# Macaron: rotated q and k are summed into the buffer that is transposed and scaled there in place; the normed tile in a two-tensor form

## The chip, the cores and the metric

The kernel runs on one core of a Trainium2 chip. The metric is the device time of one execution in microseconds. TensorE (PE), VectorE (DVE), ScalarE (ACT), GpSimd (POOL) and SyncE (SP) each work through their own instructions in order, and meet only at semaphores.

## The reference, cut to what matters

Six stages follow each other on x of shape 2 x 1024 x 128. Two of them, the first and the third, are the "macaron" stage, x + 0.5 * f(layernorm(x)), and the change is inside it. f is six layers of local attention with a gated feed-forward unit:

```python
for i in range(DEPTH):                                   # 6
    x = attn_layer(shift_tokens(x), Wqkv[i], q_scale[i], k_scale[i], Wo[i]) + x
    x = ffn_layer(shift_tokens(x), ln_g[i], ln_b[i], W1[i], b1[i], W2[i], b2[i]) + x

def attn_layer(x, Wqkv, qs, ksc, Wo):
    q, k, v = split(x @ Wqkv)                            # 16 heads of 64
    q, k = l2norm(q) * qs, l2norm(k) * ksc
    q = q * cos * scale + rotate_half(q) * sin * scale
    k = k * cos * inv + rotate_half(k) * sin * inv
    return local_attention(q, k, v) @ Wo                 # windows of 32, one back

def ffn_layer(x, g, bln, W1, b1, W2, b2):
    xn = (x - mean) / sqrt(var + 1e-05) * g + bln
    a, gate = split(xn @ W1 + b1)
    return a * gelu(gate) @ W2 + b2
```

The other four stages (linear attention, experts, softmax attention, experts) are not touched.

## The kernel before

All of x lies in SBUF, as 16 tiles of 128 tokens x 128 features. A macaron stage is one software pipeline over 96 tiles (6 layers x 16 tiles). It takes 106 steps, s = -3 to 102, and each engine has its part of `step(s)` written out by hand. In step s the engines work on several tiles at once: u = s+2 is projected to q and k and rotated, k = s+1 has its q and k transposed and its v projected, t = s goes through the softmax, o = s-1 is weighed and projected out, z = s-4 is normed for the feed-forward unit. Of each four steps three carry feed-forward matmuls for a group of four tiles (gate, up, out).

The life of q and k of one tile, with the lines of the kernel before:

- TensorE projects four pieces of 512 columns, q in pieces 0 and 1, k in pieces 2 and 3 (`project_qk`). ScalarE squares each (L534).
- VectorE rotates each piece with two multiplications by the tables (`rotate`, L640), into `turn1` and `turn2`. Piece 3 of the next tile comes behind the transposes of this one on TensorE (`turn_qk(k, 0)`, `attend(o, 1)`, `project_qk(u, 3)`).
- GpSimd adds `turn2` to `turn1`, once for q and once for k (`add`, L751).
- VectorE sums the squares (`lengths`, L645) and writes a first guess of the inverse root (L711). GpSimd refines it in twelve small instructions (`rsqrt`, L760 to L766).
- GpSimd multiplies `turn1` by these roots into `qkr` (`scale`, L744), in the next step; TensorE transposes `qkr` (`turn_qk`, L367) in four parts, 0 and 1 for q, 2 and 3 for k. Parts 1 and 2 follow each other, and `project_v` (L356) goes before part 1 and before part 3.

There is one `turn1`, `turn2` and `qkr` for q and one for k. So `rotate` of the next tile waits until `scale` has read `turn1` (semaphore `qk_rotated`), and `scale` waits until `qkr` of the tile before is transposed (`qk_turned`). L711 also waits for `scale`, since it overwrites the roots. GpSimd's order in a step is: scale q, scale k, add q, divide the softmax by its sums (L780), add k, then `rsqrt`.

The normed tile `zn` of the feed-forward unit is written by two VectorE instructions of 128 x 64 (L685 and L687), (x - mean) * root, with mean and root as one value per partition. They stand ahead of `lengths`, and so ahead of L711.

Of the kernel before, what the change touches and what calls it, by code (L numbers as in the profile page):

```python
# [13 lines left out]
ALU = mybir.AluOpType  # L14
# [7 lines left out]
P = 128  # L22
D = 128
HALF = D // 2
# [3 lines left out]
TILES = BATCH * TPB  # L28
DEPTH = 6
HEADS = 16  # L30
DH = 64
RH = DH // 2
# [9 lines left out]
LN_EPS = 1e-5  # L42
# [13 lines left out]
def slot(t):  # L56
# [8 lines left out]
             qk_rotated=2, p_turned=2, pT_kept=2, aT_kept=2, unit_gate=3, unit_up=3, gelu=3, gated=3)  # L65
# [6 lines left out]
class Counts:  # L72
# [5 lines left out]
    def part(self, n, name, i=0):  # L78
        return PARTS.get(name, 1) * (self.macaron * NT + n) + i + 1
# [17 lines left out]
def build(nc, x_in, W, const, maskc, out):  # L97
    with ExitStack() as ctx:
        def sb(name, shape, dt=F32):
            return ctx.enter_context(nc.sbuf_tensor(name, shape, dt))  # L100
# [3 lines left out]
        def sem(name):  # L104
            if name not in sems:
                sems[name] = ctx.enter_context(nc.semaphore(name))
            return sems[name]
# [6 lines left out]
        Y = sb("Y", [P, TILES, D])  # L114
# [6 lines left out]
        maskf = sb("maskf", [P, 2, NWIN])  # L121
        half = sb("half", [P, 32])
        eps = sb("eps", [P, TILES])
        spare = sb("spare", [P, 1])

        wqkv = [sb(f"wqkv{i}", [P, 3 * INNER]) for i in range(2)]
# [10 lines left out]
        turn1 = sb("turn1", [P, 2, 2, HEADS, RH])  # L137
# [81 lines left out]
        def bc(ap, n):  # L219

            return ap.unsqueeze(2).broadcast_to([ap.shape[0], ap.shape[1], n])
# [88 lines left out]
        def on(n):  # L310
            return 0 <= n < NT
# [301 lines left out]
        def macaron_dve(dve, c):  # L613
# [15 lines left out]
            def rotate(n, q):  # L629

                w, a = q // 2, q % 2
                dve.wait_ge(sem("squared"), part(n, "squared", q))
                if on(n - 1) and a == 0:
                    dve.wait_ge(sem("qk_rotated"), part(n - 1, "qk_rotated", w))
                src = bank[QK_BANK[q]][:, :].rearrange("p (h d) -> p h d", d=RH)
                for tr in range(2):
                    dst = (turn1[:, w, a, :, :], turn2[:, w, 1 - a, :, :])[tr]
                    i = a ^ tr
                    tab = ropes[:, 2 * w + tr, n % TPB, RH * i:RH * i + RH]
                    e = dve.tensor_tensor(dst, src, tab.unsqueeze(1).broadcast_to([P, HEADS, RH]), ALU.mult)  # L640
                e.then_inc(sem("turned"), 1)
# [6 lines left out]
            def step(s):  # L648
# [33 lines left out]
                if on(z):  # L682
                    if on(z - 1):
                        dve.wait_ge(sem("mixed"), mixed(s - 1))
                    dve.tensor_scalar(zn[:, 0:HALF], Y[:, z % TILES, 0:HALF], mv[:, 0:1], rn[:, 32:33], ALU.subtract,  # L685
                                      ALU.mult)
                    dve.tensor_scalar(zn[:, HALF:D], zs[:, z % 3, :], mv[:, 0:1], rn[:, 32:33], ALU.subtract,  # L687
                                      ALU.mult).then_inc(sem("unit_normed"), 1)
                if on(u):
                    lengths(u, 0)  # L690
                if on(v):
# [5 lines left out]
                    lengths(u, 1)  # L697
                if on(v):
                    dve.wait_ge(sem("unit_moments"), part(v, "unit_moments"))
                    dve.tensor_scalar(ss[:, 32:33], mv[:, 1:2], LN_EPS, None, ALU.add).then_inc(sem("unit_var"), 1)  # L700
                if on(u):
                    dve.wait_ge(sem("summed"), part(u, "summed", 1))
                    dve.tensor_scalar(ss[:, 0:32], ss[:, 0:32], 1e-24, None, ALU.max).then_inc(sem("norms_squared"), 1)
                    dve.wait_ge(sem("norms_squared"), part(u, "norms_squared"))
                if on(v):
                    dve.wait_ge(sem("unit_var"), part(v, "unit_var"))
# [28 lines left out]
        def macaron_pool(pool, c):  # L735
            at = Counts(c)
            part, mixed = at.part, at.mixed

            def scale(n, w):
                r = rn[:, 16 * w:16 * w + 16]  # L740
                pool.wait_ge(sem("added"), part(n, "added", w))
                if on(n - 1):
                    pool.wait_ge(sem("qk_turned"), part(n - 1, "qk_turned", 2 * w + 1))
                pool.tensor_tensor(qkr[:, w, :].rearrange("p (h a d) -> p a h d", a=2, d=RH), turn1[:, w, :, :, :],  # L744
                                   r.unsqueeze(1).unsqueeze(3).broadcast_to([P, 2, HEADS, RH]),
                                   ALU.mult).then_inc(sem("qk_rotated"), 1)

            def add(n, w):
                pool.wait_ge(sem("turned"), part(n, "turned", 2 * w + 1))
                t1 = turn1[:, w, :, :, :].rearrange("p a h d -> p (a h d)")  # L750
                pool.tensor_tensor(t1, t1, turn2[:, w, :, :, :].rearrange("p a h d -> p (a h d)"), ALU.add).then_inc(  # L751
                    sem("added"), 1)

            def rsqrt(s):
                n0 = NEWTON * (at.step(s) - 1)
                pool.wait_ge(sem("guessed"), at.step(s))
                for i in range(3):
                    if i:
                        pool.wait_ge(sem("newton"), n0 + 4 * i)
                    pool.tensor_tensor(rt[:, :], rn[:, :], rn[:, :], ALU.mult).then_inc(sem("newton"), 1)  # L760
                    pool.wait_ge(sem("newton"), n0 + 4 * i + 1)
                    pool.tensor_tensor(rt[:, :], rt[:, :], ss[:, :], ALU.mult).then_inc(sem("newton"), 1)  # L762
                    pool.wait_ge(sem("newton"), n0 + 4 * i + 2)
                    pool.tensor_scalar(rt[:, :], rt[:, :], -0.5, 1.5, ALU.mult, ALU.add).then_inc(sem("newton"), 1)
                    pool.wait_ge(sem("newton"), n0 + 4 * i + 3)
                    pool.tensor_tensor(rn[:, :], rn[:, :], rt[:, :], ALU.mult).then_inc(  # L766
                        sem("newton" if i < 2 else "rnorm"), 1)

            def step(s):
                u, k, t = s + 2, s + 1, s  # L770
                if on(k):
                    pool.wait_ge(sem("rnorm"), at.step(s - 1))
                    scale(k, 0)
                    scale(k, 1)
                if on(u):
                    add(u, 0)
                if on(t):
                    pool.wait_ge(sem("inverted"), part(t, "inverted"))
                    pv = prob[:, :].rearrange("p (h k) -> p h k", k=NWIN)
                    pool.tensor_tensor(pv, pv, bc(rden[:, :], NWIN), ALU.mult).then_inc(sem("normalised"), 1)  # L780
                if on(u):
                    add(u, 1)
                rsqrt(s)

            for s in range(FIRST_STEP, FIRST_STEP + STEPS):
                step(s)
# [615 lines left out]
        def _(dve):  # L1402
# [2 lines left out]
            dve.memset(gT[:, 2, :], 1.0)  # L1405
            dve.memset(half[:, :], -0.5)
            dve.memset(eps[:, :], LN_EPS)
            dve.memset(ones[:, :], 1.0)
            dve.wait_ge(sem("const_loaded"), LOADS)
            dve.tensor_copy(identb[:, :], ident[:, :])  # L1410
# [110 lines left out]
```

## Time and profile before

| What | Value |
|---|---|
| Median of 3 runs | 4565.99 us (4559.22 to 4576.77) |
| Time of the profiled execution | 4562.12 us |
| Its span | 4560.3 us |
| PE busy | 3990.9 us (88%) |
| DVE busy | 3449.5 us (76%) |
| POOL busy | 2695.7 us (59%) |
| ACT busy | 2640.0 us (58%) |
| Chain that ended last, by engine | PE 37%, DVE 33%, POOL 15%, issue 11%, ACT 3% |

How to read it: the share of busy time is that of the whole span. TensorE's matmuls are pipelined and their ends are modelled, so 88% does not say that TensorE sets the pace. The chain that ended last goes back from the last instruction, at each step to what released it. "issue" is time in which an engine waited for nothing that the profile shows. PEclk is the clock that TensorE was granted, as a share of 2.4 GHz. In rows of the timeline the columns are start (us), duration (us), engine, line, operation, output and inputs, count; a bracket tells how long the engine sat idle before and what ended that.

### The profile page before, as it was taken

What the parts mean: (1) busy time and instruction counts of PE and PEld (TensorE: products, weight loads), DVE (VectorE), ACT (ScalarE), POOL (GpSimd) and SP (SyncE); (2) the same over time, 40 slices, a digit from 0 to 9 for tenths busy, and PEclk for the clock granted to TensorE, in tenths of its full rate; (3) what the DMA queues carried; (4) which work ended last, traced back from release to release, by engine and by line L of the source; (5) the groups of instructions that cost most, each with busy time, mean ns of one, the idle gap of its engine ahead of it and who ended that gap; (6) DMA issues with size and microseconds to landing.
All of it is one profiled execution on the core that took longest, in us unless ns stands there. A gap on an engine that the chain in (4) does not pass through costs nothing.

```text
span 4560.3 us, 162200 instructions
## 1 busy us (share of the span) xinstructions
PE 3990.9 (88%) x70897; PEld 2461.2 (54%) x70897; DVE 3449.5 (76%) x5613; ACT 2640.0 (58%) x4548; POOL 2695.7 (59%) x3554
## 2 busy tenths in 40 slices
PE   4899999999999998569999999999999985899975
PEld 2566656566665656335666666565656653333333
DVE  5888888888888887468888888788888854676744
ACT  3666666666666665046666666666666641266651
POOL 4777777777777776277777777677777750100000
PEclk8999999999999999789999999999999987699996
DMA  3000000000000000000000000000000000000000
GB/s 80 5 4 24 9 23 5 9 24 9 5 24 9 23 5 9 20 3 9 4 23 9 23 4 9 23 10 23 5 9 4 5 4 0 0 1 1 1 1 9
DMA packets 75875, 53.53 MB, mean 12 GB/s; under 512 B 49048, under 2 KB 71976, under 8 KB 73520
## 3 DMA queue, kind: packets, MB, share of 16 engines
q1 hardware_dynamic: 75184, 43.29, 3.7%
q8 instruction: 560, 9.18, 0.8%
q14 instruction: 131, 1.07, 0.1%
HBM read 35.93 MB, written 1.05 MB: 8 GB/s over the span
## 4 chain that ended last, share of the span: by engine, by line
PE 37%; DVE 33%; POOL 15%; issue 11%; ACT 3%; DVEq 1%; POOLq 0%; SPq 0%; DMA 0%; ACTq 0%
DVE turn L640 12%; DVE zn L687 5%; POOL qkr L744 5%; PE psum L345 5%; PE psum L412 4%; DVE ss L645 4%; PE psum L367 3%; PE psum L1159 3%; PE psum L356 3%; PE psum L433 3%; DVE den L669 3%; POOL rt L762 2%; POOL rn L766 2%; POOL rt L760 2%; PE psum L1128 2%
## 5 line engine op out<-in xcount | busy, mean ns | idle before, releaser
L640 DVE TENSOR_TENSOR turn<-psum,ropes 128x512 f32<-128x512 f32 x1536 | 945.3, 675 | 306.3 <-POOL qkr L744 259.5
L751 POOL TENSOR_TENSOR turn<-turn 128x1024 f32<-128x1024 f32 x384 | 907.8, 2364 | 191.6 <-DVE turn L640 191.3
L345 PE MATMUL psum<-wqkv,xT 128*128 128x512 f32 x1536 | 813.8, 654 | 10.9 <-DVE turn L640 8.3
L534 ACT ACTIVATE sq<-psum 128x512 f32<-128x512 f32 x768 | 455.9, 594 | 618.1 <-PE psum L345 617.9
L744 POOL TENSOR_TENSOR qkr<-turn,rn 128x1024 f32<-128x1024 f32 x384 | 726.4, 1912 | 15.1
L367 PEld LDWEIGHTS psum<-ident,qkr 128*128 128x128 f32 x3072 | 340.0, 145 | 440.4 <-issue 158.3
L412 PEld LDWEIGHTS psum<-scratch,V 32*64 32x64 f32 x29952 | 409.6, 139 | 304.0 <-issue 302.5
L412 PE MATMUL psum<-scratch,V 32*64 32x64 f32 (+1 forms) x29952 | 461.1, 236 | 112.6 <-issue 71.7
L367 PE MATMUL psum<-ident,qkr 128*128 128x128 f32 x3072 | 479.2, 291 | 90.0 <-POOL qkr L744 87.3
L760 POOL TENSOR_TENSOR rt<-rn 128x33 f32<-128x33 f32 x636 | 156.9, 247 | 625.8 <-DVE rn L711 592.6
L356 PE MATMUL psum<-wqkv,xT 128*64 128x512 f32 x1536 | 442.7, 656 | 16.1 <-DVE turn L640 15.5
L645 DVE TENSOR_REDUCE ss<-sq 128x16 f32<-128x1024 f32 x384 | 453.7, 1184 | 0.0
L1282 DVE TENSOR_REDUCE gel<-psum 128x1 f32<-128x1024 f32 x256 | 303.9, 1220 | 154.7 <-PE psum L1128 153.8
L345 PEld LDWEIGHTS psum<-wqkv,xT 128*128 128x128 f32 x1536 | 272.4, 198 | 230.2 <-issue 196.2
L655 DVE TENSOR_REDUCE nmax<-psum 128x16 f32<-128x1024 f32 x192 | 234.9, 1223 | 210.5 <-PE psum L392 208.4
L433 PE MATMUL psum<-wo,aT 128*128 128x128 f32 x3072 | 381.0, 278 | 2.5 <-ACT aT L566 2.5
L780 POOL TENSOR_TENSOR scratch<-scratch,rden 128x1024 f32<-128x1024 f32 x192 | 365.5, 1904 | 22.1 <-DVE rden L672 22.0
L433 PEld LDWEIGHTS psum<-wo,aT 128*128 128x128 f32 x3072 | 364.4, 195 | 2.8 <-ACT aT L566 2.8
L687 DVE TENSOR_SCALAR zn<-zs,mv,rn 128x64 f32<-128x64 f32 x192 | 349.7, 1822 | 0.0
L547 ACT ACTIVATE V<-psum 128x512 f32<-128x512 f32 x384 | 229.7, 598 | 191.9 <-PE psum L356 191.5
L543 ACT ACTIVATE qT<-psum 128x512 f32<-128x512 f32 x384 | 229.1, 597 | 165.9 <-PE psum L367 165.7
L392 PEld LDWEIGHTS psum<-kT,qT 64*32 64x32 f32 x24576 | 262.8, 105 | 111.5 <-issue 90.6
(181 smaller groups left out, 6521.9 us busy)
## 6 DMA issues: line engine op xcount, KB each, us to landing
wqkv<-in_L_ffn_Wqkv_dram SPq DMA_DIRECT2D x12, 1536.0 KB, 6.9
wo<-in_L_ffn_Wo_dram SPq DMA_DIRECT2D x48, 128.0 KB, 6.7
zs<-Y SPq DMA_DIRECT2D x192, 31.8 KB
w<-in_L_ffn_W_dram SPq DMA_DIRECT2D x12, 341.0 KB
zs<-Y SPq DMA_DIRECT2D x168, 0.2 KB
w<-in_L_ffn_W_dram SPq DMA_DIRECT2D x12, 128.0 KB
rope<-in_shape_consts_dram SPq DMA_DIRECT2D x1, 1024.0 KB
X<-in_L_attn_x_dram SPq DMA_DIRECT2D x2, 512.0 KB
```

Of the source, the lines that this page charges most:

```text
L345: pe.matmul(bank[b][:, :], xT[:, n // TPB % 2, bass.ts(n % TPB, P)], wqkv[n // TILES % 2][:, INNER * w:INNER * w + INNER].rearrange("p (h ...
L356: mm = pe.matmul(bank[b][DH * e:DH * e + DH, :], xT[:, n // TPB % 2, t0:t0 + 64], wv[:, :, e, :], start=True, stop=True, skip_group_check= ...
L367: mm = pe.transpose(bank[b][:, P * j:P * j + P], qkr[:, w, P * p:P * p + P], ident[:, :])
L412: mm = pe.matmul(bank[OUT_BANK[e][x]][DH * c0:DH * c0 + DH, o0 + q0:o0 + q1], v[r0:r0 + WIN, blk // 2 % 2, p, :], pT[r0:r0 + WIN, p, q0:q1 ...
L433: mm = pe.matmul(bank[WO_BANK][:, 0:D], aT[:, p, :], wo[n // TILES % 2][:, p, :], start=(p == 0), stop=(p == PAIRS - 1))
L534: act.activation(sq[:, q // 2, q % 2, :, :], bank[QK_BANK[q]][:, :].rearrange("p (h d) -> p h d", d=RH), ACT.Square).then_inc(sem("squared ...
L640: e = dve.tensor_tensor(dst, src, tab.unsqueeze(1).broadcast_to([P, HEADS, RH]), ALU.mult)
L645: dve.tensor_reduce(ss[:, 16 * w:16 * w + 16], sq[:, w, :, :, :].rearrange("p a h d -> p h a d"), AX.XY, ALU.add).then_inc(sem("summed"), 1)
L687: dve.tensor_scalar(zn[:, HALF:D], zs[:, z % 3, :], mv[:, 0:1], rn[:, 32:33], ALU.subtract, ALU.mult).then_inc(sem("unit_normed"), 1)
L744: pool.tensor_tensor(qkr[:, w, :].rearrange("p (h a d) -> p a h d", a=2, d=RH), turn1[:, w, :, :, :], r.unsqueeze(1).unsqueeze(3).broadcas ...
L751: pool.tensor_tensor(t1, t1, turn2[:, w, :, :, :].rearrange("p a h d -> p (a h d)"), ALU.add).then_inc(sem("added"), 1)
L780: pool.tensor_tensor(pv, pv, bc(rden[:, :], NWIN), ALU.mult).then_inc(sem("normalised"), 1)
```

## The change

`add` now writes its sum straight into `qkr`, and `scale` multiplies `qkr` in place. The wait for the transposes of the tile before (`qk_turned`) moves with the write, from `scale` to `add`. `rotate` now waits for `added` of the tile before in place of `qk_rotated`. In GpSimd's step the first `add` moves behind the division of the softmax. The normed tile is written by `scalar_tensor_tensor` with the root broadcast along the row as a second tensor, and two small `tensor_scalar` instructions become `tensor_tensor` with constants in SBUF (`eps`, and a new `least`).

```diff
@@ -631,7 +632,7 @@
                 dve.wait_ge(sem("squared"), part(n, "squared", q))
                 if on(n - 1) and a == 0:
-                    dve.wait_ge(sem("qk_rotated"), part(n - 1, "qk_rotated", w))
+                    dve.wait_ge(sem("added"), part(n - 1, "added", w))
@@ -682,10 +683,11 @@
-                    dve.tensor_scalar(zn[:, 0:HALF], Y[:, z % TILES, 0:HALF], mv[:, 0:1], rn[:, 32:33], ALU.subtract,
-                                      ALU.mult)
-                    dve.tensor_scalar(zn[:, HALF:D], zs[:, z % 3, :], mv[:, 0:1], rn[:, 32:33], ALU.subtract,
-                                      ALU.mult).then_inc(sem("unit_normed"), 1)
+                    inv = rn[:, 32:33].broadcast_to([P, HALF])
+                    dve.scalar_tensor_tensor(zn[:, 0:HALF], Y[:, z % TILES, 0:HALF], mv[:, 0:1], inv, ALU.subtract,
+                                             ALU.mult)
+                    dve.scalar_tensor_tensor(zn[:, HALF:D], zs[:, z % 3, :], mv[:, 0:1], inv, ALU.subtract,
+                                             ALU.mult).then_inc(sem("unit_normed"), 1)
@@ -697,10 +699,10 @@
-                    dve.tensor_scalar(ss[:, 32:33], mv[:, 1:2], LN_EPS, None, ALU.add).then_inc(sem("unit_var"), 1)
+                    dve.tensor_tensor(ss[:, 32:33], mv[:, 1:2], eps[:, 0:1], ALU.add).then_inc(sem("unit_var"), 1)
-                    dve.tensor_scalar(ss[:, 0:32], ss[:, 0:32], 1e-24, None, ALU.max).then_inc(sem("norms_squared"), 1)
+                    dve.tensor_tensor(ss[:, 0:32], ss[:, 0:32], least[:, :], ALU.max).then_inc(sem("norms_squared"), 1)
@@ -737,19 +739,17 @@
             def scale(n, w):
-                r = rn[:, 16 * w:16 * w + 16]
+                rows = qkr[:, w, :].rearrange("p (h d) -> p h d", d=DH)
                 pool.wait_ge(sem("added"), part(n, "added", w))
+                pool.tensor_tensor(rows, rows, bc(rn[:, 16 * w:16 * w + 16], DH), ALU.mult).then_inc(
+                    sem("qk_rotated"), 1)
+
+            def add(n, w):
+                pool.wait_ge(sem("turned"), part(n, "turned", 2 * w + 1))
                 if on(n - 1):
                     pool.wait_ge(sem("qk_turned"), part(n - 1, "qk_turned", 2 * w + 1))
                 pool.tensor_tensor(qkr[:, w, :].rearrange("p (h a d) -> p a h d", a=2, d=RH), turn1[:, w, :, :, :],
-                                   r.unsqueeze(1).unsqueeze(3).broadcast_to([P, 2, HEADS, RH]),
-                                   ALU.mult).then_inc(sem("qk_rotated"), 1)
-
-            def add(n, w):
-                pool.wait_ge(sem("turned"), part(n, "turned", 2 * w + 1))
-                t1 = turn1[:, w, :, :, :].rearrange("p a h d -> p (a h d)")
-                pool.tensor_tensor(t1, t1, turn2[:, w, :, :, :].rearrange("p a h d -> p (a h d)"), ALU.add).then_inc(
-                    sem("added"), 1)
+                                   turn2[:, w, :, :, :], ALU.add).then_inc(sem("added"), 1)
@@ -772,13 +772,12 @@
-                if on(u):
-                    add(u, 0)
                 if on(t):
                     pool.wait_ge(sem("inverted"), part(t, "inverted"))
                     pv = prob[:, :].rearrange("p (h k) -> p h k", k=NWIN)
                     pool.tensor_tensor(pv, pv, bc(rden[:, :], NWIN), ALU.mult).then_inc(sem("normalised"), 1)
                 if on(u):
+                    add(u, 0)
                     add(u, 1)
```

## Rows read from the trace of the kernel before

**Rows 1.** Waits of the whole span: who waited for whom (us, times, longest).

```profile
DVE turn L640 <- POOL qkr L744: 259.5, 163, 6.0
```

**Rows 2.** Line L711 from 140 to 1789 us: count, duration, first and last start.

```profile
L711 DVE TENSOR_SCALAR rn<-ss x91: 182/183/185, 140.2 to 1788.6; 128x33 int32<-128x33 int32 x91
```

**Rows 3.** Busy time by engine of the same stretch, granted clock, DMA.

```profile
140.20:1788.60 1648.40, 1545.92 (x31559) 997.27 (x31558) 1370.75 (x2194) 1069.49 (x1821) 1206.86 (x1530) 0.96 0.05 13
```

**Rows 4.** Timeline of VectorE, one step, L711 to L711.

```profile
158.10 0.18 DVE L711 TENSOR_SCALAR rn<-ss 128x33 int32<-128x33 int32 x1
...
164.29 2.48 DVE L640 TENSOR_TENSOR turn<-psum,ropes 128x512 f32<-128x512 f32 x4 [3.22 <-POOL qkr L744]
...
167.93 0.25 DVE L672 RECIPROCAL rden<-den 128x16 f32<-128x16 f32 x1
168.10 2.42 DVE L640 TENSOR_TENSOR turn<-psum,ropes 128x512 f32<-128x512 f32 x4
170.43 0.22 DVE L678 BATCH_NORM_STATS2 st<-Y 128x6 f32<-128x64 f32 x1
...
170.69 0.44 DVE L685 TENSOR_SCALAR zn<-Y,mv,rn 128x64 f32<-128x64 f32 x1
171.05 2.40 DVE L687 TENSOR_SCALAR zn<-zs,mv,rn 128x64 f32<-128x64 f32 x1
173.37 1.21 DVE L645 TENSOR_REDUCE ss<-sq 128x16 f32<-128x1024 f32 x1
...
176.03 0.18 DVE L711 TENSOR_SCALAR rn<-ss 128x33 int32<-128x33 int32 x1
```

**Rows 5.** Timeline of GpSimd, the same step, its four large pieces.

```profile
162.27 3.78 POOL L744 TENSOR_TENSOR qkr<-turn,rn 128x1024 f32<-128x1024 f32 x2
166.85 2.37 POOL L751 TENSOR_TENSOR turn<-turn 128x1024 f32<-128x1024 f32 x1 [0.80 <-DVE turn L640]
169.18 1.91 POOL L780 TENSOR_TENSOR scratch<-scratch,rden 128x1024 f32<-128x1024 f32 x1
171.04 2.37 POOL L751 TENSOR_TENSOR turn<-turn 128x1024 f32<-128x1024 f32 x1
```

**Rows 6.** Timeline of TensorE, the same step: transposes of q and k.

```profile
164.33 0.63 PE L367 MATMUL psum<-ident,qkr 128*128 128x128 f32 x4 [1.94 <-POOL qkr L744]
...
166.99 1.08 PE L356 MATMUL psum<-wqkv,xT 128*64 128x512 f32 x4
168.00 1.09 PE L367 MATMUL psum<-ident,qkr 128*128 128x128 f32 x8
```

**Rows 7.** Timeline of ScalarE, the same step.

```profile
164.99 0.60 ACT L543 ACTIVATE qT<-psum 128x512 f32<-128x512 f32 x1 [2.35 <-PE psum L367]
...
167.09 0.60 ACT L534 ACTIVATE sq<-psum 128x512 f32<-128x512 f32 x1
```

**Rows 8.** Lines L685 and L687: duration min/median/max in ns, first and last.

```profile
L685 DVE TENSOR_SCALAR zn<-Y,mv,rn x192: 294/434/2434, 152.8 to 3749.1; 128x64 f32<-128x64 f32 x192
...
L687 DVE TENSOR_SCALAR zn<-zs,mv,rn x192: 300/2399/2416, 153.1 to 3749.3; 128x64 f32<-128x64 f32 x192
```

**Rows 9.** Timeline of VectorE, three steps earlier, before the first normed tile.

```profile
109.42 0.18 DVE L711 TENSOR_SCALAR rn<-ss 128x33 int32<-128x33 int32 x1
...
124.80 0.18 DVE L711 TENSOR_SCALAR rn<-ss 128x33 int32<-128x33 int32 x1
```

**Rows 10.** Timeline at a layer's start: VectorE's row, then GpSimd's.

```profile
321.66 2.76 DVE L624 TENSOR_TENSOR ropes<-rope,qks 128x256 f32<-128x256 f32 x8
...
321.68 2.83 POOL L764 TENSOR_SCALAR rt<-rt 128x33 f32<-128x33 f32 x1
```

**Rows 11.** Line L764: duration min/median/max in ns, first and last start.

```profile
L764 POOL TENSOR_SCALAR rt<-rt x636: 222/223/2881, 53.9 to 3767.3; 128x33 f32<-128x33 f32 x159
```

**Rows 12.** Timeline of TensorE, transposes of the last of 89 steps.

```profile
1778.23 0.66 PE L367 MATMUL psum<-ident,qkr 128*128 128x128 f32 x4
1781.93 1.09 PE L367 MATMUL psum<-ident,qkr 128*128 128x128 f32 x8
```

More of the change, by code:

```diff
@@ L123, in build @@
         eps = sb("eps", [P, TILES])
+        least = sb("least", [P, 32])
         spare = sb("spare", [P, 1])
@@ L1407, in _ @@
             dve.memset(eps[:, :], LN_EPS)
+            dve.memset(least[:, :], 1e-24)
             dve.memset(ones[:, :], 1.0)
```

## Prediction

> **What bounds the kernel now.** I read the list of waits first. The longest wait of VectorE inside the macaron stage is that of the rotations (L640) for GpSimd's scaling (L744), 259.5 us in 163 waits [rows 1]. This is the wait that the change aims at. The question is what it is part of. L711 runs once in each step, so its starts give the pace: 91 of them lie between 140.2 and 1788.6 us [rows 2], which is 1648.4 / 90 = 18.32 us a step. The second macaron stage repeats the pattern, so about 180 steps count. TensorE is busy for 1545.92 us of that stretch [rows 3], 17.18 us a step. It is close to the pace, but it also idles 1.94 us ahead of its first transposes, for the same scaling [rows 6].
>
> Then I followed one step on the timeline, from L711 at 158.10 to L711 at 176.03, 17.93 us. All times from here count from the first L711. Scaling starts at +4.17 [rows 5], the rotations wait for it until +6.19 [rows 4], GpSimd adds q at +8.75, divides the softmax at +11.08 and adds k at +12.94 [rows 5]. VectorE has its normed tile ready to write at +12.59. The first half (L685) takes 0.44 us, the second (L687) 2.40 us, from +12.95 to +15.35 [rows 4]. GpSimd's add of k lasts 2.37 us from +12.94 [rows 5], the same time to a hundredth. The next L711 is 176.03 - 173.37 = 2.66 us behind the start of L645, which follows the normed tile [rows 4]. So the pace is a loop: L711, roots, scaling, rotations, normed tile held until GpSimd's add ends, lengths, L711. The unheld L687 takes 0.30 us at the least, and half of all take about 2.40 [rows 8]; where L687 is quick, L685 is as a rule the long one (up to 2434 ns [rows 8]): one of the two is held by one large GpSimd instruction in nearly all steps. Before the first normed tile the loop takes 124.80 - 109.42 = 15.38 us [rows 9]. Two waits are in the loop, then: for the scaling, and for GpSimd's add. The change takes the first away. What counts is whether the second one goes too.
>
> **The rotations' wait: removed.** Rotation of q no longer waits until +6.19; it can go on when the softmax has been centred, some 3 us earlier (3.22 us idle [rows 4]). Pieces 0 to 2 are early. Piece 3 is not: its projection stands behind the first transposes on TensorE, which still wait for the scaling, at +6.23 [rows 6]. ScalarE squares it from +8.99 for 0.60 us [rows 7], so piece 3 starts at about +9.66, takes half of 2.42 us [rows 4] and then 170.69 - 170.43 = 0.26 us of statistics [rows 4]. VectorE wants to write the normed tile at +11.1, 1.5 us sooner than before.
>
> **The add: it gets a new wait.** GpSimd's order is now scale, scale, divide, add q, add k. Scaling ends at +7.9, the sums are inverted by then (rotations 0 and 1 were early), and dividing ends at +9.8 (1.91 us [rows 5]). But add q writes `qkr`, so it waits for part 1 of the transposes of the tile before. Part 0 starts at +6.23 and ScalarE sees it 164.99 - 164.33 = 0.66 us later [rows 6, 7]; part 1 starts at 168.00 [rows 6], +9.90. With 0.66 us, and 0.06 us taken for GpSimd's own start, add q begins at +10.62, not at +9.8. Add k follows 2.32 us later (171.04 - 169.18 = 1.86 is the same spacing for a 1.91 us instruction, so 2.37 - 0.05), at +12.94. That is exactly where it is today. Wherever the normed tile is still held by this add, L711 comes again at +17.93, and nothing is won.
>
> **Does the two-tensor form free the normed tile?** No row shows a VectorE instruction of this form beside a large add of GpSimd. The nearest row is at a layer's start: eight VectorE `tensor_tensor` with both inputs in SBUF (L624) run for 2.76 us, and GpSimd's L764, issued 0.02 us behind them, takes 2.83 us [rows 10] where half of its kind take 223 ns or less [rows 11]. So two SBUF inputs on VectorE and GpSimd exclude each other, at least in this direction. The new form has two SBUF inputs, the tile and the broadcast root. I take it as held as today, 2.40 us; the other end is 0.30 us [rows 8]. In its unheld length I see no difference (bounds -0.1 to +0.1 us a step from the 0.30). The two small `tensor_tensor` come when GpSimd idles: nothing, and at most a wait for the end of an add, inside the next paragraph's bounds.
>
> The Trainium skill has a rule for both sides. "SBUF — State Buffer", § Who interferes with whom, says that a VectorE instruction with two SBUF inputs contends with a GpSimd instruction that reads SBUF, and the later one blocks until the first ends. By it the form is held as before. "VectorE: DVE Perf Modes", § Why `tensor_tensor` can't do 2×_2P or 4×, says that an instruction with two tensors has no mode that takes both ports for one; who reads only that page expects the form to run free, as in the first rival. Rows 10 speak for the first page in one direction; the other direction no row shows.
>
> **What the new wait costs.** Before, TensorE's transposes of part 1 could be late without harm: nothing in the loop waited for them. Now every delay between part 0 and part 1 goes into add q, add k, the held normed tile and L711. In the step above part 1 is 3.67 us behind part 0 [rows 6], in the last one 3.70 [rows 12]. Over the 89 steps from one to the other the distance is below 3.8 us in 39, between 3.8 and 5.4 in 32, above in 18; the mean is 4.63. The excess comes from pauses inside the small attention matmuls and from stretches at the lower of the two clocks (granted mean 0.96 [rows 3]). So a step costs 17.93 + (4.63 - 3.67) = 18.89 us. Layer starts add 2.76 us [rows 10] in 5 of 90 steps, as they do today: 0.15. Against that, where TensorE is slow behind the projection of piece 3, or parts 1 and 3 lie more than 2.4 us apart, a gap opens on GpSimd and the whole normed tile slips through. By the same rows that is so in about 14 of 89 steps, worth up to 2.66 us each: -0.41. Sum: 18.89 + 0.15 - 0.41 = 18.63 us, against 18.32, +0.31 us a step. Times 180: +56 us. The profiled execution took 4562.12 us, 4 us below the median of the runs. Forecast: 4618 us.
>
> **Other edits.** The sum costs between 1.91 us (one input broadcast, L744 and L780) and 2.37 us (two full inputs, L751) [rows 5]; I take 2.37, since it has two. The strided write costs nothing visible: L744 has it today and half of its 3.78 us is no more than L780's 1.91 [rows 5]. The scaling in place has L780's shape. GpSimd's total stays. The moved wait queues add q, add k and the roots behind the transposes; the division stands ahead of it, so TensorE's transposes of the softmax don't suffer.
>
> **Rivals.**
> 1. The two-tensor form runs free. Then L711 is ready at about +14.3 and GpSimd sets the loop: add k ends at +15.3, roots may start there instead of at +0.26, 15.0 + 0.96 = 16.0 us. But TensorE's busy time of 17.18 us a step [rows 3] is more than that. With 0.4 us for its waits, 17.6 us: -0.72 x 180 = -130 us, 4432. For it: the form isn't today's. Against it: rows 10. It decides as soon as the held length of L687 falls below 1 us. Chance 0.25.
> 2. The form is held, but VectorE comes first. It wants to write at +11.1 and add q begins at +10.62. Were it 0.8 us earlier, both halves would fit into GpSimd's wait. Same price, 4432. Chance 0.04.
> 3. TensorE's delays don't reach the loop, since pauses merely move into waits that get longer. A step then costs 17.93 + 0.15 + up to 0.25 of what disturbs today's loop: 18.08 to 18.33, 4519 to 4564; I take 4560. Chance 0.16.
> 4. At the far end of the forecast itself, no tile slips through: 19.04 us, +130 us, 4692.
>
> **How the numbers follow.** The forecast has chance 0.55, its own range is 4585 to 4695. The range of 8 in 10 has to take in half of the free form: 4425 to 4695. A measurement of this kernel can tell about 0.5% from no change, 4543 to 4589. Faster: rivals 1 and 2 and the low edge of 3, 0.31. Same: most of rival 3 and the low edge of the forecast, 0.18. Slower: 0.51.
>
> **What would show it.** In the changed profile the waits of L640 for the scaling are gone, and the line of the add shows idle time released by the transposes (L367). The second half of the normed tile still has a median near 2.4 us. L711 comes every 17.9 us in undisturbed steps. If the normed tile's halves are both near 0.3 us, rival 1 or 2 holds: 2 if add q starts after them. If the idle time ahead of the add is small and the pace is 18.1 to 18.3 us, rival 3 does.

## The result, and the profile after

| | Before | After |
|---|---|---|
| Median | 4562.6 us (4551.6 to 4576.8) | 4720.2 us (4704.6 to 4727.8) |
| Ratio | 1 | 1.034 (95%: 1.030 to 1.038) |
| Span of the profiled execution | 4560.3 us | 4702.8 us |
| First / second macaron stage, first to last of 91 roots | 1648.4 / 1649.9 us | 1709.3 / 1725.3 us |

The change makes the kernel 3.4% slower. The forecast was 4618 us, 1.2% slower. The direction was right, the size too small by about 100 us, and the result lies above both the range of the forecast (4585 to 4695) and that of 8 in 10. Both stages together account for 60.9 + 75.4 = 136 of the 142.5 us by which the span grew.

Waits of the whole span, after (engine and line, whom it waited for; us in total, times, longest):

```profile
POOL qkr L751 <- PE psum L368: 273.0, 155, 4.7
DVE turn L641 <- ACT sq L535: 268.1, 123, 5.8
POOL scratch L778 <- DVE rden L673: 179.5, 135, 11.6
```

For comparison, two of the same waits before:

```profile
DVE turn L640 <- ACT sq L534: 45.7, 50, 4.5
POOL scratch L780 <- DVE rden L672: 22.0, 3, 12.2
```

The wait of the rotations for the scaling, 259.5 us [rows 1], is gone from the list. In its place GpSimd's add waits 273.0 us for the transposes, and the rotations wait 268.1 us for the squares, where it was 45.7 us before. By the timeline nearly all of it stands ahead of piece 3, as the prediction had it. GpSimd's division waits 179.5 us for its sums, where it was 22.0 us before.

The line of the first guess, L711 before and L713 now, in the first and in the second macaron stage (count, duration min/median/max in ns, first and last start):

```profile
L713 DVE TENSOR_SCALAR rn<-ss x91: 182/182/2328, 140.6 to 1850.0; 128x33 int32<-128x33 int32 x91
...
L713 DVE TENSOR_SCALAR rn<-ss x91: 182/183/2235, 2102.9 to 3828.1; 128x33 int32<-128x33 int32 x91
```

(1850.0 - 140.6) / 90 = 18.99 us a step, against 18.32 [rows 2]. Busy time of the engines over the same stretch, after (columns as in [rows 3]):

```profile
140.70:1850.00 1709.30, 1570.73 (x31548) 1004.65 (x31525) 1482.30 (x2195) 1067.74 (x1820) 1207.95 (x1530) 0.95 0.05 12
```

VectorE is busy 111.55 us more than in [rows 3], GpSimd 1.09 us more. The two lines of the normed tile, after, over the whole span:

```profile
L687 DVE SCALAR_TENSOR_TENSOR zn<-Y,mv,rn x192: 264/2054/2452, 153.2 to 3880.8; 128x64 f32<-128x64 f32 x192
...
L689 DVE SCALAR_TENSOR_TENSOR zn<-zs,mv,rn x192: 271/2396/2427, 155.6 to 3881.0; 128x64 f32<-128x64 f32 x192
```

The second half is held as before (median 2396 ns). The first half is now held too: median 2054 ns, where it took 0.44 us in the step of [rows 4].

One undisturbed step, from L713 at 256.11 to L713 at 274.16, after. Timeline of VectorE (start, duration, engine, line, operation, operands, count):

```profile
256.11 0.18 DVE L713 TENSOR_SCALAR rn<-ss 128x33 int32<-128x33 int32 x1
...
264.57 2.44 DVE L641 TENSOR_TENSOR turn<-psum,ropes 128x512 f32<-128x512 f32 x4
...
267.19 2.06 DVE L687 SCALAR_TENSOR_TENSOR zn<-Y,mv,rn 128x64 f32<-128x64 f32 x1
269.17 2.40 DVE L689 SCALAR_TENSOR_TENSOR zn<-zs,mv,rn 128x64 f32<-128x64 f32 x1
...
274.16 0.18 DVE L713 TENSOR_SCALAR rn<-ss 128x33 int32<-128x33 int32 x1
```

The same step on GpSimd:

```profile
260.28 3.76 POOL L744 TENSOR_TENSOR qkr<-qkr,rn 128x1024 f32<-128x1024 f32 x2
264.73 1.90 POOL L778 TENSOR_TENSOR scratch<-scratch,rden 128x1024 f32<-128x1024 f32 x1 [0.69 <-DVE rden L673]
266.80 4.68 POOL L751 TENSOR_TENSOR qkr<-turn 128x1024 f32<-128x1024 f32 x2 [0.17 <-PE psum L368]
```

And TensorE's transposes, parts 0, then 1 and 2:

```profile
262.33 0.63 PE L368 MATMUL psum<-ident,qkr 128*128 128x128 f32 x4 [0.20 <-POOL qkr L744]
...
266.00 1.09 PE L368 MATMUL psum<-ident,qkr 128*128 128x128 f32 x8
```

Part 0 is at +6.22 and part 1 at +9.89. Add q begins at +10.69 (forecast +10.62) and VectorE could write the normed tile at +11.08 (forecast +11.1). The first half is held until add q ends, the second until add k ends. L713 comes back at +18.05, where [rows 4] have 17.93. In this step the time that the rotations won is spent waiting inside L687.

### The profile page after: what moved, and what is told of

The parts are those of the page before. It is cut to its first block, busy times and chain, and to the rows that moved or that the text cites. A ratio compares the mean times of both kernels' runs of the same rounds, so it can differ in the third digit from the quotient of the medians.

```text
span 4702.8 us, 162391 instructions
## 1 busy us (share of the span) xinstructions
PE 4056.0 (86%) x70897; PEld 2478.4 (53%) x70897; DVE 3680.2 (78%) x5614; ACT 2637.5 (56%) x4548; POOL 2696.5 (57%) x3554
## 4 chain that ended last, share of the span: by engine, by line
PE 37%; DVE 31%; POOL 13%; issue 12%; ACT 5%; DVEq 1%; SPq 0%; POOLq 0%; DMA 0%; ACTq 0%
DVE zn L689 7%; DVE zn L687 6%; PE psum L346 5%; DVE turn L641 5%; PE psum L413 5%; POOL qkr L744 5%; PE psum L368 4%; DVE ss L646 4%; PE psum L1158 3%; PE psum L357 2%; PE psum L1127 2%; POOL rn L766 2%; POOL rt L762 2%; POOL rt L760 2%; PE psum L499 2%
## 5 line engine op out<-in xcount | busy, mean ns | idle before, releaser
L641 DVE TENSOR_TENSOR turn<-psum,ropes 128x512 f32<-128x512 f32 x1536 | 952.9, 674 | 271.2 <-ACT sq L535 268.1
L751 POOL TENSOR_TENSOR qkr<-turn 128x1024 f32<-128x1024 f32 x384 | 901.0, 2365 | 297.1 <-PE psum L368 273.0
L346 PE MATMUL psum<-wqkv,xT 128*128 128x512 f32 x1536 | 829.1, 664 | 9.4 <-DVE turn L641 4.9
L744 POOL TENSOR_TENSOR qkr<-qkr,rn 128x1024 f32<-128x1024 f32 x384 | 722.4, 1902 | 15.0
L778 POOL TENSOR_TENSOR scratch<-scratch,rden 128x1024 f32<-128x1024 f32 x192 | 365.1, 1902 | 179.6 <-DVE rden L673 179.5
L357 PE MATMUL psum<-wqkv,xT 128*64 128x512 f32 x1536 | 456.0, 675 | 0.0
L689 DVE SCALAR_TENSOR_TENSOR zn<-zs,mv,rn 128x64 f32<-128x64 f32 x192 | 363.8, 1895 | 0.0
```

The costliest lines, as they stand in the source:

```text
L346: pe.matmul(bank[b][:, :], xT[:, n // TPB % 2, bass.ts(n % TPB, P)], wqkv[n // TILES % 2][:, INNER * w:INNER * w + INNER].rearrange("p (h ...
L357: mm = pe.matmul(bank[b][DH * e:DH * e + DH, :], xT[:, n // TPB % 2, t0:t0 + 64], wv[:, :, e, :], start=True, stop=True, skip_group_check= ...
L689: dve.scalar_tensor_tensor(zn[:, HALF:D], zs[:, z % 3, :], mv[:, 0:1], inv, ALU.subtract, ALU.mult).then_inc(sem("unit_normed"), 1)
L744: pool.tensor_tensor(rows, rows, bc(rn[:, 16 * w:16 * w + 16], DH), ALU.mult).then_inc(sem("qk_rotated"), 1)
```

## The experiments

"Step" is the mean of 90 steps of one macaron stage, the first and then the second, in the profiled execution. The other columns are of the first stage. "Part 0" is the mean time from the start of the scaling to the first transposes, and "undisturbed" the length of a step in which TensorE shows no pauses. All are worked out from the timelines, in us.

| Kernel | Step, first / second stage | Part 0 | Part 1 - part 0 | Undisturbed |
|---|---|---|---|---|
| before | 18.32 / 18.33 | 2.50 | 4.64 | 17.92 |
| after | 18.99 / 19.17 | 2.40 | 4.63 | 18.05 |
| E1 moves alone | 19.05 / 19.11 | 2.62 | 4.82 | 18.0 |
| E2 form alone | 18.36 / 18.39 | 2.43 | 4.62 | 17.98 |
| E3 after, accumulator form | 17.84 / 17.85 | 3.16 | 4.63 | 15.54, 16.5 to 17.2 |
| E4 before, accumulator form | 17.85 / 17.72 | 4.47 | 4.72 | 15.76, 16.4 to 17.3 |
| E12 E3 with the small ones back | 17.61 / 17.64 | 3.14 | 4.48 | 15.48, 16.5 to 17.2 |
| E5 after, two buffers | 18.66 / 18.82 | 2.53 | 4.77 | 17.13, 17.6 to 18.1 |
| E7 after, old order | 21.18 / 21.03 | 4.59 | 4.72 | 17.60, 19.6 to 21.3 |
| E10 two buffers, old order | 18.25 / 18.00 | 2.72 | 4.82 | 17.15 |
| E6 two buffers, accumulator form | 17.68 / 17.60 | 3.95 | 4.60 | 14.6, 16.4 to 18.4 |
| E8 before, normed on ScalarE | 17.62 / 17.98 | 4.75 | 4.59 | 15.40, 16.6 to 17.4 |
| E9 after, normed on ScalarE | 17.81 / 17.75 | 3.21 | 4.68 | 15.47, 17.0 to 17.1 |

Where two values stand in the last column, the first is that of the one step in four whose scores have no feed-forward matmuls ahead of them on TensorE, and the second that of the others.

### E1 and E2: the moves without the form, and the form without the moves

E1 is the changed kernel with the old one-tensor forms, E2 the kernel before with the new ones. The core of E1's edit (the first half and the two small instructions change in the same way):

```diff
-                    dve.scalar_tensor_tensor(zn[:, HALF:D], zs[:, z % 3, :], mv[:, 0:1], inv, ALU.subtract,
-                                             ALU.mult).then_inc(sem("unit_normed"), 1)
+                    dve.tensor_scalar(zn[:, HALF:D], zs[:, z % 3, :], mv[:, 0:1], rn[:, 32:33], ALU.subtract,
+                                      ALU.mult).then_inc(sem("unit_normed"), 1)
```

> The changed kernel with the one-tensor form of the normed tile and of the two small instructions put back; the moved add, the in-place scaling, the wait for the transposes and GpSimd's new order stay. Theory (VectorE's normed tile is held by GpSimd's add in either form, the new wait of the add for the transposes is the loss): ratio to before 1.03 to 1.04, as the whole change; undisturbed step 18.0 us; one half of the normed tile at 2.4 us. Rival (the two-tensor form is what costs): 1.01 or less.

Measured: 4710.2 us against 4587.1, ratio 1.026 (1.018 to 1.034).

> The kernel before with the two-tensor form alone. Theory (held in either form): within 0.5% of before, second half of the normed tile still near 2.4 us, undisturbed step 17.9 us. Rival (the form runs free of GpSimd): both halves near 0.3 us, undisturbed step near 15.6 us, about 3% faster.

Measured: 4591.7 us, ratio 1.002 (0.998 to 1.005). The source line of the second half, E1 and then E2:

```profile
L688 DVE TENSOR_SCALAR zn<-zs,mv,rn x192: 301/2398/2458, 155.7 to 3892.1; 128x64 f32<-128x64 f32 x192
```

```profile
L689 DVE SCALAR_TENSOR_TENSOR zn<-zs,mv,rn x192: 270/2396/2414, 154.0 to 3758.4; 128x64 f32<-128x64 f32 x192
```

Both forms are held alike, 2398 and 2396 ns in the median. The loss is in the moves. The profiled execution of E1 takes 3435.1 us for the 2 x 90 steps, the whole change 3434.6. The intervals of the two ratios overlap (1.018 to 1.034 and 1.030 to 1.038), so that a small share of the form beside the moves is not excluded.

### E3, E4 and E12: take the hold away

The old form with an accumulator output, in the changed kernel (E3) and in the kernel before (E4). The accumulator changes what is written, so the normed tile of both, and with it the output, is not that of the reference. All waits stay. The second half in E3 (the first has column 0 of `sink`):

```diff
+                    dve.tensor_scalar(zn[:, HALF:D], zs[:, z % 3, :], mv[:, 0:1], rn[:, 32:33], ALU.subtract,
+                                      ALU.mult, accum_out=sink[:, 1:2]).then_inc(sem("unit_normed"), 1)
```

> The changed kernel, with the normed tile written by the one-tensor instruction that also puts out its accumulator. By the Trainium skill (SBUF - State Buffer, Who interferes with whom) that form has no two-port mode and should not be held. Theory (the hold is what passes the add's wait on to the next step): both halves near 0.3 us, undisturbed step 15.1 to 17.2 us set by TensorE, mean step about 17.6 us instead of 18.99, about 3% faster than before (4430). Rival (the wait for the transposes sets the pace by itself, hold or no hold): mean step 18.5 us or more, 1.01 to before or slower.

Measured: 4464.9 us, ratio 0.974 (0.966 to 0.982).

> The kernel before with that same accumulator form of the normed tile, nothing else. Theory (the hold is 2.1 to 2.3 us of each 17.92 us step and nothing else is late): undisturbed step 15.6 to 16 us, mean step 16.9 to 17.5 us as TensorE's 17.2 us of work comes to bind, 4350 to 4430 us, 3 to 5% faster. Rival (another wait takes its place at once, since TensorE idles little): less than 1% faster.

Measured: 4485.8 us, ratio 0.979 (0.971 to 0.986), less than expected: the mean step is 17.85 us, not 16.9 to 17.5. Timeline of E3, both engines:

```profile
1014.74 0.32 DVE L687 TENSOR_SCALAR_CACHE_REDUCE zn<-Y,mv,rn 128x64 f32<-128x64 f32 x1
1014.99 0.08 DVE L687 DVE_READ_ACCUMULATOR zn<-Y,mv,rn 128x1 f32 x1
1014.99 0.33 DVE L689 TENSOR_SCALAR_CACHE_REDUCE zn<-zs,mv,rn 128x64 f32<-128x64 f32 x1
...
1017.58 1.49 DVE L702 TENSOR_TENSOR ss<-mv,eps 128x1 f32<-128x1 f32 x1
...
1014.35 4.70 POOL L751 TENSOR_TENSOR qkr<-turn 128x1024 f32<-128x1024 f32 x2 [1.72 <-PE psum L369]
```

The normed tile is written in 0.3 us beside a running add. With the hold gone the changed kernel is 5% faster than with it, and the two kernels have the same step, 17.84 and 17.85 us. The reason is TensorE: the undisturbed step falls to 15.5 to 15.8 us only where no feed-forward matmuls stand ahead of the scores, and in three steps of four it is 16.4 to 17.3 us. Busy time of E4 in 500 us (columns as in [rows 3]):

```profile
1000.00:1500.00 500.00, 476.36 (x9855) 309.90 (x9843) 377.40 (x744) 332.55 (x567) 373.71 (x470) 0.97 0.04 11
```

It is busy for 476 of 500 us. Part 0 in E4 lies 4.47 us behind the start of the scaling, not 2.50: TensorE comes to its first transposes some 2 us after the scaling could have released them. So the wait of the rotations that the change removes is worth nothing here.

The one-column L702 took 1.49 us in the rows above, held by the add as well. E12 is E3 with the small ones in their old form:

```diff
-                    dve.tensor_tensor(ss[:, 32:33], mv[:, 1:2], eps[:, 0:1], ALU.add).then_inc(sem("unit_var"), 1)
+                    dve.tensor_scalar(ss[:, 32:33], mv[:, 1:2], LN_EPS, None, ALU.add).then_inc(sem("unit_var"), 1)
```

> The changed kernel with the accumulator form of the normed tile (its output is not the reference's), and the two small instructions in the one-tensor form again. In the run with the two-tensor form a single column (output 128x1) took 1.50 us of VectorE beside GpSimd's add. Theory (two SBUF inputs make VectorE wait for GpSimd's add, whatever the size): that line is back at about 0.14 us, the next one, 128x32, may be held in its place; same time within 0.5%. Rival (the 1.50 us have another cause): the line stays at 1.4 to 1.5 us.

Measured in a single run: 4464.2 us, as E3. (In the profiled execution the step is 17.61 us, not 17.84, and what comes behind the second stage takes longer, so that only the whole agrees; the four runs of E3 lie 40 us apart.) Source lines of E12:

```profile
L702 DVE TENSOR_SCALAR ss<-mv x192: 135/143/154, 138.1 to 3626.4; 128x1 f32<-128x1 f32 x192
...
L705 DVE TENSOR_SCALAR ss<-ss x192: 180/1384/2293, 62.2 to 3573.3; 128x32 f32<-128x32 f32 x192
```

and of E3:

```profile
L702 DVE TENSOR_TENSOR ss<-mv,eps x192: 146/1317/2358, 140.3 to 3673.0; 128x1 f32<-128x1 f32 x192
...
L705 DVE TENSOR_TENSOR ss<-ss,least x192: 177/179/2404, 63.0 to 3622.9; 128x32 f32<-128x32 f32 x192
```

The one-column one-tensor form is never held here (154 ns at the most), and its two-tensor form is. Taking the hold off L702 only hands it to L705 behind it.

### E5, E7 and E10: the new wait, and the order

E5 gives `qkr` a second buffer, so that the add waits for the transposes of two tiles before (the edit that makes room for the buffer is left out here):

```diff
-                if on(n - 1):
-                    pool.wait_ge(sem("qk_turned"), part(n - 1, "qk_turned", 2 * w + 1))
+                if on(n - 2):
+                    pool.wait_ge(sem("qk_turned"), part(n - 2, "qk_turned", 2 * w + 1))
```

> The changed kernel with two buffers for the rotated q and k, so that the add waits for the transposes of the tile before last, which are long done. To make room, the rotary tables are scaled in place in every layer instead of from a copy: the same work, but the tables and the output come out other than the reference's. Theory (the add's wait for the transposes is the loss; the normed tile stays held): the waits of the add for the transposes are gone, undisturbed step 17.1 us, mean step 17.7 to 18.3 us, ratio to before 0.97 to 1.00. Rival (the loss is elsewhere, for instance in GpSimd's order): ratio stays near 1.03.

Measured: 4641.9 us, ratio 1.009 (1.006 to 1.012), between the two expectations. Waits of E5 on GpSimd:

```profile
POOL scratch L782 <- DVE rden L677: 228.6, 148, 11.9
```

The wait for the transposes is gone, and a step falls from 18.99 to 18.66 us, by 0.33 (by 0.35 in the second stage). The rest has another cause: the division waits longer for its sums (228.6 us, after 179.5), with add q behind it. An undisturbed step took 17.13 to 17.3 us where no feed-forward matmuls stood ahead of the scores, and 17.6 to 18.1 us where they did. E7 and E10 put add q ahead of the division again, E7 in the changed kernel and E10 in E5:

```diff
+                if on(u):
+                    add(u, 0)
                 if on(t):
                     pool.wait_ge(sem("inverted"), part(t, "inverted"))
...
                 if on(u):
-                    add(u, 0)
                     add(u, 1)
```

> The changed kernel with GpSimd's old order: the add of q ahead of the division of the softmax. Theory (the add waits for TensorE's transposes until about 10.6 us into the step, and whatever is queued behind it on GpSimd waits too): the division ends at about 14.9 instead of 9.8 us, the add of k ends about 2 us later, undisturbed step 19.5 to 20 us, ratio to before 1.08 or more. Rival (the order was a matter of taste, and the move of the division cost as much as it gave): within 1% of the changed kernel, 1.03 to before.

Measured: 5096.3 us, ratio 1.105 (1.102 to 1.108). The undisturbed step is 17.60 us without feed-forward matmuls ahead of the scores and 19.6 to 21.3 us with them, where 19.5 to 20 was expected. Waits of E7:

```profile
POOL qkr L751 <- PE psum L368: 1153.2, 188, 14.7
...
PEld psum L426 <- POOL scratch L780: 493.4, 190, 2.7
```

With one buffer the old order closes a longer loop. Add q waits for the transposes, the division behind it comes late, and TensorE waits for the division. The other order, then, is something that the change needs, not a part that could be undone.

> The kernel with two buffers (rotary tables scaled in place, so the output is not the reference's), and GpSimd's old order on top: the add of q ahead of the division. With two buffers alone the ratio was 1.009 and the mean step 18.66 us; in steps whose scores stand behind feed-forward matmuls the division waited for its sums and the add behind it. Theory (that order is the rest of the loss): the add of q starts right behind the scaling in all steps, undisturbed steps 17.1 to 17.2 us of every kind, mean step 17.7 to 18.2 us, ratio 0.97 to 0.99. Rival (the rest is lost elsewhere, the order is harmless once the transposes are not waited for): within 0.3% of 1.009.

Measured: 4536.1 us against 4599.3, ratio 0.989 (0.984 to 0.995). A step takes 18.25 us in the first stage and 18.00 in the second, and an undisturbed one 17.15 us of any kind. From the changed kernel to E5 the new wait gives back 0.33 us a step (second stage 0.35), from E5 to E10 the order gives back 0.41 (second stage 0.82). What is left of the change is then a gain, 18.32 - 18.25 = 0.07 us a step in the first stage and 18.33 - 18.00 = 0.33 us in the second, though 0.8 us in an undisturbed step. Over the whole kernel the runs are 1.1% faster than before. So the early add pays once it has a buffer of its own and its old place in the order. With the one buffer, and the new order that this buffer asks for, it costs more than it gives.

### E6: both obstacles away

E5 with the accumulator form.

> Two buffers and the accumulator form together (output not the reference's): neither the wait for the transposes nor the hold is left. Theory (TensorE with 17.2 us of work and its own pauses binds then): mean step 17.5 to 17.9 us, no more than 0.5% below the accumulator form alone (4465). Rival (the wait for the transposes still costs when nothing is held): 1% or more below it.

Measured in a single run: 4430.4 us, 0.8% below E3 and E12, between the two expectations. The stages tell more. The two macaron stages and what comes behind them, E6 and then E12 (columns as in [rows 3]):

```profile
140.10:1731.50 1591.40, 1517.90 (x31558) 984.88 (x31558) 1237.65 (x2374) 1067.35 (x1821) 1206.27 (x1530) 0.97 0.05 13
1988.20:3572.20 1584.00, 1512.17 (x31559) 983.84 (x31558) 1243.21 (x2374) 1067.32 (x1821) 1203.30 (x1530) 0.98 0.05 12
3572.20:4428.60 856.40, 657.87 (x4266) 316.18 (x4264) 487.79 (x744) 374.53 (x691) 88.05 (x164) 0.86 0.01 2
```

```profile
140.20:1725.20 1585.00, 1511.55 (x31550) 981.06 (x31541) 1299.31 (x2375) 1066.82 (x1820) 1211.19 (x1530) 0.98 0.05 13
1987.10:3574.70 1587.60, 1513.57 (x31570) 983.86 (x31569) 1298.55 (x2374) 1069.26 (x1824) 1213.51 (x1531) 0.97 0.05 12
3574.70:4462.40 887.70, 690.88 (x4260) 326.84 (x4258) 487.52 (x744) 375.69 (x690) 88.34 (x164) 0.82 0.01 2
```

The 2 x 90 steps take 3175.4 us in E6 and 3172.6 us in E12, but 3211.9 us in E3, and the difference of 34 us between the whole of E6 and of E12 lies almost wholly behind them (856.4 against 887.7 us), in stages that no edit touches, at a granted clock of 0.86 against 0.82. As the four runs of E3 lie 40 us apart, a single run of E6 can't tell whether the wait for the transposes still costs anything once nothing is held: not settled.

### E8 and E9: the normed tile on ScalarE

ScalarE computes root * x + (-mean * root) with the same inputs, in the kernel before (E8) and in the changed kernel (E9):

```diff
+                act.activation(shift[:, 0:1], mv[:, 0:1], ACT.Copy, scale=rn[:, 32:33]).then_inc(sem("shift_a"), 1)
...
+                act.activation(shift[:, 1:2], shift[:, 0:1], ACT.Copy, scale=-1.0).then_inc(sem("shift_b"), 1)
...
+                act.activation(zn[:, 0:HALF], Y[:, z % TILES, 0:HALF], ACT.Identity, bias=shift[:, 1:2],
+                               scale=rn[:, 32:33])
+                act.activation(zn[:, HALF:D], zs[:, z % 3, :], ACT.Identity, bias=shift[:, 1:2],
+                               scale=rn[:, 32:33]).then_inc(sem("unit_normed"), 1)
```

> The kernel before with the normed tile written by ScalarE, which reads (x * root - mean * root) in the gap ahead of its copy of the first transposes; VectorE's two instructions are gone. Theory (the hold on VectorE is 2.1 to 2.3 us of the step, and TensorE's work takes over as the bound): undisturbed step with no feed-forward work 15.3 us, mean step 17.3 to 17.9 us, ratio 0.95 to 0.98. Rival (four more instructions on ScalarE delay the squares that the rotations wait for): 0.99 or slower.

Measured: 4481.5 us, ratio 0.972 (0.969 to 0.976). Timeline of ScalarE, E8:

```profile
1004.37 0.28 ACT L548 ACTIVATE shift<-mv,rn 128x1 f32<-128x1 f32 x1
1004.68 0.20 ACT L550 ACTIVATE shift<-shift 128x1 f32<-128x1 f32 x1
1004.98 0.44 ACT L554 ACTIVATE zn<-Y,shift,rn 128x64 f32<-128x64 f32 x1
1005.33 0.43 ACT L556 ACTIVATE zn<-zs,shift,rn 128x64 f32<-128x64 f32 x1
```

> The changed kernel (its two small instructions in the one-tensor form again) with the normed tile on ScalarE in the same way. Theory (once nothing holds the normed tile, GpSimd's wait for the transposes is off the loop, and TensorE binds as in the kernel before with that edit): mean step 17.3 to 17.9 us, ratio 0.95 to 0.98, within 0.5% of the other one. Rival (the moved add gives its gain only now): 1% or more below the other one.

Measured: 4482.7 us, ratio 0.974 (0.969 to 0.979). Some 1.35 us of ScalarE (0.28 + 0.20 + 0.44 + 0.43) replace 2.8 us of VectorE before (0.44 + 2.40) and 4.5 us after (2.06 + 2.40). On this ground the moves of the change are worth nothing that these runs can show: the intervals overlap, and the 2 x 90 steps take 3204.6 and 3200.2 us. E8 computes what the reference does and is faster than both kernels, by 2.8% and by about 6%.

## Why the prediction was right and where it was wrong

**The hold stays: right.** The held length of 2.40 us was carried over from the form of before, on the ground of the one direction that [rows 10] show, and L689 measured 2396 ns. E2 confirms it without the moves. The Trainium skill, "SBUF — State Buffer", § Who interferes with whom, states the hold for two SBUF inputs, and this case's runs agree down to one column (L702 in E3, median 1317 ns, against 143 ns in the one-tensor form in E12). One reading of the prediction was a little too sharp: the held half of 2.40 us and the add of 2.37 us [rows 4, 5] agree to 0.03 us, not to a hundredth.

**The new wait: right in place and size.** Add q at +10.69 for +10.62, the undisturbed step 18.05 for 17.93. GpSimd's sum took 2362 ns in the median of L751 (forecast 2.37), and scaling in place 1.9 us each. Part 1 came 4.63 us behind part 0 in the mean, as in the forecast. The signs named in advance are there: the old wait gone, the new one present, L689 near 2.4 us.

**The size, forecast 18.63 us a step, measured 18.99 in the first stage: the credit for slips was the term that failed.**

1. The slip credit of -0.41 us was mis-sized. It assumed that a step in which the normed tile slips through is a plain gain. Of 90 steps 22 have at least one half free, called a slip below (12 both; 14 were forecast). One such step and the step behind it, after. VectorE:

```profile
218.56 0.18 DVE L713 TENSOR_SCALAR rn<-ss 128x33 int32<-128x33 int32 x1
...
231.54 0.27 DVE L687 SCALAR_TENSOR_TENSOR zn<-Y,mv,rn 128x64 f32<-128x64 f32 x1
231.72 2.39 DVE L689 SCALAR_TENSOR_TENSOR zn<-zs,mv,rn 128x64 f32<-128x64 f32 x1
...
236.71 0.18 DVE L713 TENSOR_SCALAR rn<-ss 128x33 int32<-128x33 int32 x1
```

TensorE's transposes in this step and the next:

```profile
224.78 1.09 PE L368 MATMUL psum<-ident,qkr 128*128 128x128 f32 x4 [2.17 <-POOL qkr L744]
230.81 1.09 PE L368 MATMUL psum<-ident,qkr 128*128 128x128 f32 x8
...
243.89 0.66 PE L368 MATMUL psum<-ident,qkr 128*128 128x128 f32 x4
```

GpSimd:

```profile
231.61 4.75 POOL L751 TENSOR_TENSOR qkr<-turn 128x1024 f32<-128x1024 f32 x2 [3.25 <-PE psum L368]
...
240.87 3.76 POOL L744 TENSOR_TENSOR qkr<-qkr,rn 128x1024 f32<-128x1024 f32 x2
```

Part 1 is late, 230.81 - 224.78 = 6.03 us behind part 0. Half a tile slips through, and the step takes 18.15 us all the same. But what made it slip is that TensorE is late, and it is late in the next step too. There the scaling starts at 240.87, part 0 follows only at 243.89, 3.02 us behind, not 2.05 as in the undisturbed step, and the step takes 19.40 us (256.11 - 236.71).

Over all 90 steps: what follows part 1 takes 5.39 us in a step with a slip and 8.21 in the others. That is 0.69 us a step, more than the credit. But part 0 comes 3.42 us behind the scaling in a step that follows a slip and 2.07 us otherwise, which costs 22 x 1.35 / 90 = 0.33 us a step. In 5 steps, each behind one with both halves free, the scaling itself starts at +6.2 to +6.3 instead of +4.17, since GpSimd is still at add k when L713 has run: another 0.12. A step that follows a slip takes 20.47 us in the mean. Net, the slips are worth 0.69 - 0.33 - 0.12 = 0.24 us, not 0.41: two thirds of the gain is paid back one step later.

2. In a step without a slip, what follows part 1 was forecast at 8.03 us (17.93 - 9.90). It took 8.16 in the undisturbed step and 8.21 in the mean: +0.18. The distance from the scaling to part 0, taken from one step at 2.06 us, is 2.40 in the mean, but nearly all of the difference is that of the steps behind a slip, counted above.

The difference to 18.99 then comes to 0.17 for the slips, 0.18 for the rest behind part 1 and 0.01 for part 0: 0.36 of 0.36. That part 1 - part 0 matched is in part luck. The forecast took its mean from the kernel before, and the second stage did not keep to it. There it is 4.94 us, 0.31 more than in the first, and the scaling is 0.15 later, as 22 steps have both halves free; what follows part 1 is 0.32 shorter. So the step is 0.18 us longer, 19.17. Why TensorE is later there is open. In the first stage the rise is 33 us above the forecast's 28, in the second 47: together the 80 us by which the rise in the two stages (136 us) is above the forecast's 56.

**Rivals.** The fourth, no tile slips through, at 19.04 us and 4692 us, comes nearest to the measured time, though its condition was not met, as 22 of 90 steps have a slip. I gave it no chance of its own and set the upper end of the range at its value, so nothing above it was left for the missing terms. The first would have been worth its price: with the hold removed (E3) the kernel runs at 0.974 of before, or 4446 us, against 4432 forecast, and TensorE sets its pace, at 17.84 and not at 17.6 us (17.61 in the single run of E12). The third, that TensorE's delays don't reach the loop, is refuted by 18.99 us. The second came true in single steps: both halves fit into GpSimd's wait in 12 of 90 steps and in 22 of 90 of the second stage. The price set on it did not follow, as the next step pays most of it back.

**A step I called free.** I argued that the division, ahead of the wait, would not suffer. The division did come early (+8.62 in the undisturbed step, not +11.08), but the order costs add q: between E5 and E10 it is worth 0.41 us a step in the first stage and 0.82 in the second, once the transposes don't cover it. In the changed kernel they cover it: add q starts 0.85 us behind part 1 in the mean and 0.80 undisturbed.

**Left open.** Why TensorE pauses and why it does so more in the second stage, about 6 us of the span outside the two stages, 16 us by which the median of the runs after lies above their profiled execution, and E6.

## What to carry to other kernels

When a buffer is written earlier, its wait for the last reader moves earlier too: work out who the new writer waits for, and take the mean of every distance in the new loop, not one step's. A step that escapes a hold because another engine is late keeps only part of the gain (here a third), since that engine is still late in the next step. Where a VectorE instruction with a tile and a per-partition value in SBUF lies beside large GpSimd work, moving it to ScalarE was worth more here (2.8%) than removing a wait and keeping the hold (1.1% at best, E10).

## What was not expected of the hardware

Two VectorE instructions in a row may each be held by one of two GpSimd instructions in a row: L687 until add q ended (2.06 us), L689 until add k ended (2.40 us), one slot at each handover. The one-column form with two SBUF inputs was held for 1317 ns in the median (E3), in its one-tensor form not at all (143 ns, E12), while the 128x32 one-tensor form is held (median 1384 ns, E12). The accumulator form of the same 128x64 instruction runs beside GpSimd in 0.33 us, plus 0.08 us for reading the accumulator.
